# Last tile of tokens listed by a product of 0/1 rows on TensorE instead of by indirect DMAs, and the tile ahead of it routed inside attention's last values product

## What is computed

```
x = x + L0_xattn(layernorm(x), ctx, wq, wk, wv, wo)
x = x + L0_ffn(layernorm(x), w_gate, wi_0, wi_1, wo)        # 8 experts, 2 per token, I = 256
x = x + L1_xattn(layernorm(x), ctx, mask)                   # softmax(x ctx^T / sqrt(D)) ctx
x = x + L1_ffn(layernorm(x), gate_w, w_gate, w_up, w_down)  # 32 experts, 8 per token, I = 192

# a mixture of experts: logits -> top K -> weights; for a chosen expert
y = (silu(x @ gate_e) * (x @ up_e)) @ down_e                # weighted and summed per token
```

## Time and profile before

| | |
|---|---|
| median of 3 runs | 956.7 us (955.2 to 958.67) |
| the profiled execution's own time | 963.59 us |
| its span, first to last instruction | 961.8 us |
| TensorE matmul busy | 776.8 us (81%) |
| VectorE / ScalarE busy | 535.9 / 517.3 us |
| GpSimd busy | 455.7 us |
| `list_tokens` (L1013), all | 84.6 us in 80 indirect DMAs |
| mean granted TensorE clock | 0.927 of full speed |

### The profile page before, as it was taken

One profiled execution on the slowest core, in us unless ns is written; L12 is line 12 of the kernel. 1 busy time (PEld: TensorE's weight loads), 2 busy tenths in 40 slices (PEclk: granted clock), 3 DMA queues, 4 the chain that ended last, 5 costly groups with the idle time before them and its releaser, 6 DMA issues.

```text
span 961.8 us, 19102 instructions
## 1 busy us (share of the span) xinstructions
PE 776.8 (81%) x5216; PEld 433.3 (45%) x5217; DVE 535.9 (56%) x1504; ACT 517.3 (54%) x782; POOL 455.7 (47%) x373
## 2 busy tenths in 40 slices
PE   3999999999838989367699715989889889898880
PEld 2444455554424545134355303555555555555540
DVE  5553445565453555165688541674675764566642
ACT  6533244544445765223555423777687777677650
POOL 3882000000142667420067774566776766667760
PEclk9999999999958999779799856999999999999995
DMA  8562200100045797791111105799899999999778
GB/s 281 179 217 94 66 33 23 35 23 34 29 132 152 191 250 140 175 324 65 44 46 47 46 15 156 193 280 257 219 257 285 259 258 229 245 240 237 143 135 284
DMA packets 108780, 151.89 MB, mean 158 GB/s; under 512 B 18464, under 2 KB 59680, under 8 KB 108736
## 3 DMA queue, kind: packets, MB, share of 16 engines
...
...
...
## 4 chain that ended last, share of the span: by engine, by line
PE 48%; DMA 12%; issue 12%; DVE 12%; ACT 6%; DVEq 3%; ACTq 3%; POOL 2%; SPq 2%; POOLq 0%
PE pst L191 39%; DMA x_rows<-xT,row_no 4%; PE pst L1285 4%; DVE big L1172 3%; DMA big<-in_L_ffn_wo_dram 2%; PE pst L506 2%; DMA mid<-moe_normalised_rows,row_no 2%; POOL moe_tokens_of_experts L1013 2%; ACT mid L1321 1%; ACTq L1184 1%; DVE mid L1399 1%; DMA big<-x_rows 1%; ACT big L1165 1%; PE pst L1258 1%; DVEq L1177 1%
## 5 line engine op out<-in xcount | busy, mean ns | idle before, releaser
L191 PE MATMUL pst<-big,mid 128*128 (+1 forms) x1392 | 273.0, 347 | 39.7 <-DVE big L1172 24.0
L1013 POOL DMA_INDIRECT moe_tokens_of_experts<-token_no,small x80 | 84.6, 1057 | 274.0 <-DVE small L1066 253.9
L191 PEld LDWEIGHTS pst<-big,mid 128*128 128x128 f16 x1392 | 133.1, 98 | 146.5 <-issue 55.0
L1285 PE MATMUL pst<-big,mid 128*128 x520 | 129.9, 383 | 1.9 <-ACT mid L1332 1.4
L1321 ACT ACTIVATE mid<-pst 128x1024 f16<-128x1024 f16 x102 | 104.4, 1024 | 41.4 <-PE pst L1258 40.0
L1474 POOL DMA_INDIRECT x_rows<-mid,row_no x50 | 93.7, 1874 | 50.7 <-DMA x_rows<-xT,row_no 19.8
L1474 POOL DMA_INDIRECT x_rows<-xT,row_no x50 | 90.6, 1812 | 55.3 <-DMA x_rows<-mid,row_no 17.3
L1399 DVE SCALAR_TENSOR_TENSOR mid<-pst,small,mid 128x192 f32<-128x192 f32 (+1 forms) x100 | 42.7, 427 | 120.3 <-ACT mid L1327 120.2
L191 PE MATMUL pst<-ctxN,mid 128*128 128x512 f16 x384 | 91.8, 399 | 3.2 <-ACT mid L632 3.2
L1464 POOL DMA_INDIRECT xT<-moe_normalised_rows,row_no x54 | 59.6, 1104 | 37.4 <-issue 15.3
L1170 DVE TENSOR_TENSOR big<-big (+2 forms) x40 | 74.6, 1865 | 3.8 <-issue 0.2
...
## 6 DMA issues: line engine op xcount, KB each, us to landing
...
```

The lines of the kernel that those rows point to most:

```text
L191: last = nc.tensor.matmul(dst, stationary(a, c), moving(b, c), start=(k == 0), stop=(k == 3 * len(parts) - 1))
L1013: nc.gpsimd.indirect_dma_start(out=self.tab_d[:, :], out_offset=bass.IndirectOffsetOnAxis(ap=self.addr[j % 2][:, k:k + 1], axis=0), in_=to ...
L1285: last = nc.tensor.matmul(bank(6 + p), hT[:, k, :], self.d[:, s, h, c, :], start=(q == 0), stop=(q == len(seq) - 1))
```

## The change

- The listing by indirect DMA goes over tiles 0 to 6 only. Tile 7 is listed by a matrix product: `decode` takes each of its K addresses apart into a slot (a row of the table, 0 to 127) and a column; `slots_hot` makes K matrices 128 x 128 with the token's value where column number and slot agree, and zero elsewhere; `columns_hot` makes K matrices of 0/1 over the table's columns (64 in the first layer, 256 in the second); `list_last` multiplies them on TensorE and adds the K products up in PSUM bank 0. `tab16` becomes table plus this product. `table_sp` waits for the listings of three odd tiles instead of four.
- In the second layer, `logits` of tile 6 run behind 9 and `rank` of tile 6 behind 18 of the 24 matmuls of `values(7)`, instead of behind it and behind `norm_turn(7)`. VectorE's `choose`, `weight` and `place` of tile 6 stand ahead of `update(7)`. On ScalarE `soften(6)`, `store_weights(5)` and `store_weights(6)` stand ahead of `norm_high(7)`.
- In both layers `weight(7)` moves from ahead of `place(7)` to behind `columns_hot`; the four small operations on `ftab`, `ti` and `nquad` move behind the wait for `route_pe` 3; `sel` moves behind `tab16`; `split_lo(0)` moves behind the first four `rows_in_turn`.
- GpSimd's four stores of spare rows (L1487, L1488) move from behind the last listing to behind the listing of tile 0 (`spare_rows`).
- Constants: `tile_row` is 16-bit, `part_no` has a column more, `col_no` (column numbers, 16-bit) and `place_no` are new, `stats` has two rows instead of eight. The ring of raw weight buffers is as before.

```
-        tile_row = sb("tile_row", [P, 112], F32)
-        part_no = sb("part_no", [P, 2], F32)
+        tile_row = sb("tile_row", [P, 112], F16)
+        part_no = sb("part_no", [P, 3], F32)
         row_no = sb("row_no", [P, 8], I32)
-        spare16 = sb("spare16", [1, P], F16)
+        col_no = sb("col_no", [P, 2 * P], F16)
+        place_no = sb("place_no", [P, 3, 8], I32)
...
+        def three(pe, dst, parts, stationary, moving, pauses=None):
             k, last = 0, None
             for c in parts:
+                if pauses and c in pauses:
+                    pauses[c]()
...
+                    if not self.first and i == NT - 1:
+                        self.values(pe, i, {3: lambda: self.next.logits(pe, i - 1), 6: lambda: self.next.rank(pe, i - 1)})
+                    else:
+                        self.values(pe, i)
...
-                self.next.rank(pe, NT - 2)
+                if self.first:
+                    self.next.rank(pe, NT - 2)
                 self.next.logits(pe, NT - 1)
                 self.next.rank(pe, NT - 1)
...
+                else:
+                    self.next.soften(act, NT - 2)
+                    self.next.store_weights(act, NT - 3)
+                    self.next.store_weights(act, NT - 2)
+                    self.next.norm_high(act, NT - 1)
                     self.next.norm_move(act, NT - 1, self.norm_bank(NT - 1))
                 self.next.soften(act, NT - 1)
...
+                else:
+                    self.next.choose(dve, NT - 2)
+                    self.next.weight(dve, NT - 3)
+                    self.next.place(dve, NT - 2)
+                    self.next.weight(dve, NT - 2)
+                    self.update(dve, NT - 1)
+                    self.next.norm_row(dve, NT - 1)
+                    self.next.norm_low(dve, NT - 1)
                 self.next.choose(dve, NT - 1)
-                self.next.weight(dve, NT - 1)
                 self.next.place(dve, NT - 1)
...
-                    sp.wait_ge(self.listed[q], 16 * NT // 2 * self.K)
+                    sp.wait_ge(self.listed[q], 16 * (NT // 2 - q) * self.K)
...
+            def decode(self, dve):
+                L, K, src = self.E.bit_length() - 1, self.K, self.addr[(NT - 1) % 2][:, 0:self.K]
+                slot, col, rest = (place_no[:, r, 0:K] for r in range(3))
+                fslot, fcol, value = (place_no[:, r, 0:K].bitcast(F32) for r in range(3))
+                dve.wait_ge(self.addr_s, self.b + NT)
+                nc.vector.tensor_scalar(slot, src, L, P - 1, ALU.arith_shift_right, ALU.bitwise_and)
+                nc.vector.tensor_scalar(col, src, L + 7, L, ALU.arith_shift_right, ALU.logical_shift_left)
+                link(dve, nc.vector.tensor_scalar(rest, src, self.E - 1, None, ALU.bitwise_and))
+                nc.vector.tensor_copy(fslot, slot)
+                link(dve, nc.vector.tensor_tensor(fcol, col, rest, ALU.add))
+                link(dve, nc.vector.tensor_scalar(value, fslot, -1.0, part_no[:, 0:1], ALU.mult, ALU.add))
+            def slots_hot(self, dve):
+                for k in range(self.K):
+                    slot, value = (place_no[:, r, k:k + 1].bitcast(F32) for r in (0, 2))
+                    nc.vector.tensor_scalar(self.one_slot[:, k, :], col_no[:, 0:P], slot, value, ALU.is_equal, ALU.mult)
+            def columns_hot(self, dve):
+                for k in range(self.K):
+                    last = nc.vector.tensor_scalar(self.one_col[:, k, :], col_no[:, 0:NT * self.E],
+                                                   place_no[:, 1, k:k + 1].bitcast(F32), None, ALU.is_equal)
+                last.then_inc(self.rows_s, 1)
+            def list_last(self, pe):
+                pe.wait_ge(self.rows_s, 1)
+                for k in range(self.K):
+                    last = nc.tensor.matmul(bank(0)[:, 0:NT * self.E], self.one_slot[:, k, :], self.one_col[:, k, :],
+                                            start=(k == 0), stop=(k == self.K - 1))
+                last.then_inc(self.route_pe, 1)
...
+                self.list_last(pe)
                 pe.wait_ge(self.tab_s, 3)
                 nc.tensor.matmul(bank(4)[:, 320:320 + NE], ones16[0:1, :], self.crow, start=True, stop=True).then_inc(self.route_pe, 1)
-                pe.wait_ge(self.rows_s, 1)
+                pe.wait_ge(self.rows_s, 2)
                 for q in range(self.NQ):
...
             def dve_route(self, dve):
+                self.decode(dve)
                 dve.wait_ge(self.route_pe, 1)
                 nc.vector.tensor_scalar(self.nt16, self.cnt2, 1.0, None, ALU.max).then_inc(self.tab_s, 1)
+                self.slots_hot(dve)
                 dve.wait_ge(self.route_pe, 2)
                 link(dve, nc.vector.tensor_copy(self.incl, b4[0:E, 4:5]))
                 nc.vector.tensor_scalar(self.past, tile_row[0:E, :], self.incl, None, ALU.is_ge).then_inc(self.tab_s, 1)
+                self.columns_hot(dve)
+                self.weight(dve, NT - 1)
                 dve.wait_ge(self.route_pe, 3)
                 passed, earlier = b4[0:1, 64:64 + NE], b4[0:1, 192:192 + NE]
                 link(dve, nc.vector.scalar_tensor_tensor(self.colrow, earlier, -1.0, tile_row[0:1, :], ALU.mult, ALU.add))
                 link(dve, nc.vector.scalar_tensor_tensor(self.colrow, self.colrow, float(E), passed, ALU.mult, ALU.add))
+                nc.vector.memset(self.ftab[:, 0:3], 0)
...
                 nc.vector.scalar_tensor_tensor(self.crow, self.over, 4096.0, self.colrow, ALU.mult, ALU.add).then_inc(self.tab_s, 1)
+            def dve_rows(self, dve):
+                NE, b4 = self.NE, bank(4)
                 dve.wait_ge(self.route_pe, 4)
+                dve.wait_ge(self.tab_in, 32)
+                nc.vector.scalar_tensor_tensor(self.tab16, self.tab, float(-NT * P), bank(0)[:, 0:NT * self.E], ALU.add,
+                                               ALU.add).then_inc(self.rows_s, 1)
+                dve.wait_ge(self.route_pe, 5)
                 for q in range(self.NQ):
+                    nc.vector.tensor_scalar(self.sel[:, q, :], b4[:, 320:320 + NE], part_no[:, q + 1:q + 2], None, ALU.is_equal)
+                dve.wait_ge(self.route_pe, 6)
                 nc.vector.tensor_copy(self.tabT[0:self.CQ, :, :], bank16(3)[0:self.CQ, 0:self.NQ * P].rearrange("p (q s) -> p q s", q=self.NQ)).then_inc(self.rows_s, 1)
-                dve.wait_ge(self.route_pe, 6)
+                dve.wait_ge(self.route_pe, 7)
+                link(dve, nc.vector.tensor_scalar(self.rows, bank(5)[:, 0:NE], float(NT * P), None, ALU.add))
...
                 self.dve_route(dve)
-                self.split_lo(dve, 0)
                 self.dve_rows(dve)
                 for t in range(4):
                     self.rows_in_turn(dve, t, t)
+                self.split_lo(dve, 0)
...
+            def spare_rows(self, pool):
+                pool.wait_ge(self.before, 1)
                 for q in range(2):
                     pool.dma_start(acc_d[q][NT * P:NT * P + P // 2, :], x_sb[0:P // 2, 0, :]).then_inc(self.scat[q], 16)
                     pool.dma_start(acc_d[q][NT * P + P // 2:(NT + 1) * P, :], x_sb[P // 2:P, 0, :]).then_inc(self.scat[q], 16)
+            def pool(self, pool):
...
-            for j in range(NT):
+            for j in range(NT - 1):
                 exp0.list_tokens(pool, j)
+                if j == 0:
+                    exp0.spare_rows(pool)
```

68 lines of the change are left out of this document (29 added, 39 removed).

## The result

| | before | changed |
|---|---|---|
| median, timed side by side | 958.7 us (955.2 to 964.1, 8 runs) | 951.0 us (948.1 to 955.6, 8 runs) |
| the profiled execution's own time | 963.6 us | 951.7 us |
| its span | 961.8 us | 949.9 us |
| mean granted TensorE clock | 0.927 | 0.933 |

The ratio is 0.9915, interval 0.9891 to 0.9938: faster, by 7.7 us. The forecast was 12.7 us and 944.0, with a range to 949.0; the time lies outside it.

What follows compares the result with a forecast made beforehand. It took two holes between attention and experts as the target: GpSimd's listing in the second layer, VectorE's chain in the first. Gains of 11.4 + 1.3 = 12.7 us gave 950.9, less 0.7% 944.0 us; range 941.0 to 949.0.

Steps and rivals of the forecast that it cites:

- a term put at nothing: Next loads of weights, both layers: start 7.7 and 3.3 us later relative to the first gather, at no cost.
- Update(7) and the root: Second layer, VectorE: `update(7)` about 1.5 us later, the root's 1.28 us table load just hidden; 1.6 later in all.
- The table and VectorE: Second layer: table ready at 569.7, VectorE at 570.6, so VectorE last by 0.9; row numbers 12.6 us earlier.
- The one-hot operations: Second layer, VectorE: the 16 operations of `slots_hot` and `columns_hot` take 4.0 us, bounds 2.5 to 5.2.
- The shared port pair: Second layer: `slots_hot` and `columns_hot` hold tile 6's eighth listing at most 2.8 us; up to 945.9; 20% together with Dearer.
- Gathers beside `split_lo(0)`: Second layer: GpSimd's first gather is delayed 1.2 us by the moved split, with 0 to 2.9 possible.
- The first layer: Row numbers 2.1 us earlier, gather 1.3 lost, about 0.5 back from the next weights' load; 1.3 us gained in all.
- Dearer: VectorE's 16 operations take 5.2 us or more and splits hold gathers fully: 948.0 us; 20% together with The shared port pair.
- Cheap: VectorE's 0/1 operations take 2.5 us, the table is last and no gather is held: 942.5 us; 15%.
- The loop gives back: Experts' loop: weight loads sit otherwise against gathers and scatters, and late loads are waited for: 948 to 950 us; 10%.
- Slower than before: TensorE's clock falls after the idle matmuls because the first gather comes too late; five low-clock tiles cost 13 us; 3%.
- No change: The table still waits for something as late as tile 7's listing; VectorE would need 13 us more than counted; 2%.

Runs made afterwards that it cites:

- c_before: The kernel before with only the experts' list stored as 16-bit instead of 32-bit; ratios to before 1.0028, 1.0032 and 1.0025 in three sets.
- e_root_first: The changed kernel with 16-bit list, next round's loads held back, and `store_weights(6)` behind `norm_high(7)` in the second layer; 947.89 us, ratio 0.9878.
- e_early_split: The changed kernel with 16-bit list, next round's loads held back, and expert 0's splits early in the second layer; 943.43 us, ratio 0.9834.
- e_both: `e_early_split` with `store_weights(6)` also behind `norm_high(7)`; 966.58 us, ratio 0.9914, in a set about 15 us slower for every kernel.
- e_both2: The kernel of `e_both` measured again in the third set; 944.94 us, ratio 0.9832.

## Why the prediction was wrong

**The time.** By the stages the mechanism was right, and the change won 13.6 us where the sum has 12.7. The time was not: 7.7 us instead of 12.7, and 951.0 instead of 944.0. Two steps failed.

The first is the last of the sum, "The three runs have a median of 956.7, 0.7% under the profiled one, so I subtract there". Eight runs of before have 958.7, and the larger sets 960.9, 959.7 and 960.0: 2.0 us of the miss of 7.0 are this base. The range, 8 us wide, took in the rivals' costs and nothing for runs of one kernel that lie 9 us apart.

The second is a term put at nothing: "the next loads of weights ... are wanted only when an expert of the ring's next round is split, more than 15 us later". It asks when the data is needed, not what it travels beside. In the kernel before, the load stood behind the table's load in SyncE's list and went out 11.95 us ahead of the first gate matmul of the second layer; now `split_lo(0)` releases it 6.9 us ahead of it, upon the gathers. Held back, it gives 3.0 us by the stages, and the kernel has 948.5 us, inside the range. In the first layer the sum even took 0.5 us as a gain.

That the stages come to 13.6 all the same is in part luck: the 3.0 us are made up by row numbers that came 1.5 us earlier than forecast (13.5 against 12.6 in the second layer, 2.65 against 2.1 in the first) and by gates which, with the loads held, lie 0.2 us behind before's in the second layer and 0.6 ahead of them in the first, where the sum had 1.2 and 0.8 behind.

What is left of the miss, 5.0 us less in the difference of medians than the sum has, is not explained, for the stages, with the cost of the loads in them, won more than the sum. The difference of medians is 7.7 us in the first measurement, 9.2 and 10.7 in the later sets, 11.8 and 12.8 between controls that both have the 16-bit list, while the mean spans of the traces differ by 13.1. Of these 13.1, 2.4 are draws: the traced executions of before lie 4.9 and 2.7 us above and 1.8 below their kernel's median, those of the change 0.7 above, 3.0 below and 0.9 above. `c_before` was 0.25 to 0.32% over before in all three sets; no stage of its traces is longer for it, but of before itself there is only one trace, and a slow one. Why is open, and with it whether the real difference is nearer 8 or 13 us.

**Update(7) and the root.** Predicted 1.5 later, and the root's table load "just hidden", 1.6 in all. A root that its table load holds up was one of the prediction's signs of being wrong, and it came. Measured 0.45, and VectorE waited 1.22 us for the root where it had waited 0.27 (`e_root_first` undoes that). ScalarE in time, against the earlier trace rows:

```profile
553.78 0.32 ACT L1141 ACTIVATE big<-big,small 128x32 f32<-128x32 f32 x1 [1.90 <-DMA moe_normalised_rows<-big]
554.13 0.33 ACTq L1144 DMA_DIRECT2D moe_normalised_rows<-big  x1
554.49 1.28 ACT L305 ACT_TABLE_LOAD   x1 [0.39 <-ACT big L1141]
555.78 0.20 ACT L305 ACTIVATE std<-rstd 128x1 f32<-128x1 f32 x1
```

The store of tile 5's weights is waited for until 553.78 and the load ends at 555.77, which less 2.03 is 553.74, as forecast (554.0); but VectorE had the variance at 554.79, or 552.76, 1.1 us earlier than forecast, and waits. The sum of both, 1.4, is near the 1.6; that two terms of the wrong size add up to it is luck.

**The table and VectorE.** Tile 6's listing, the 1.26 us rhythm and the load 2.16 us behind the last listing came as forecast. VectorE was last in the changed kernel; with `e_root_first` the table is last by 0.59, so the two are level within a microsecond, as the sum had them (0.9). Row numbers 13.5 us earlier over three traces against 12.6: `columns_hot` ended at 569.19, or 567.16 less the 2.03, 0.9 earlier than forecast, most of it because the group itself took 1.64 us and not 2.4, while `slots_hot` took 0.4 more than forecast.

**The one-hot operations.** 3.66 us against 4.0, inside the bounds of 2.5 to 5.2. The parts are the other way about: operations of 128 columns with two pointers start 0.22 us apart, those of 256 columns with one pointer 0.20. In the first layer, with no listing beside them, the two-pointer ones again start 0.22 us apart and one-pointer ones of 64 columns 0.15: 192 columns more cost 0.05 us, or 0.26 ns each. The tiers of "VectorE: DVE Perf Modes" in the Trainium skill gave an estimate of 1.8 us. On the rate the trace agrees, for at the 0.96 GHz of that page 0.26 ns are four columns a cycle; the fixed part is what the estimate had too small (0.06 us, where the trace leaves 0.13 with one pointer and 0.19 with two).

**The shared port pair.** In the changed kernel this rival did not come: the listing issued at 566.38, within `slots_hot`, took 0.97 us. In the kernels where a listing began just behind the start of `columns_hot`, it took 1.35 to 1.55 us and ended with the group (above). For these one-pointer operations the trace agrees with the Trainium skill's "SBUF — State Buffer", on the engine ports, though the hold costs 0.4 to 0.6 us and not the 2.8 at most that the rival had; beside `slots_hot` the listings of all traces took 0.95 to 1.13.

**Gathers beside `split_lo(0)`.** The row of before was right. A gather that was issued beside the `tensor_tensor` took 1.62 us in the second layer and 2.13 in the first, and 0.99 with the split out of the way; a listing took 2.27 in before, 2.38 in `e_early_split`, 2.44 in `e_both` and 1.35 in `e_both2`. All six ended 0.27 to 0.31 us ahead of the end of the split's second half, whenever they had been issued, so the split holds them nearly to its end rather than slowing them by a fixed amount; a listing issued 0.03 us ahead of the split in `e_both2` took 0.96. The same page of the Trainium skill says, as an inference, that such an operation leaves descriptor writing alone; six measurements here differ. I took 1.2 us for the gather of the second layer, and the extra in the row is 0.6. The sum also left out that this gather goes out 1.24 us behind the row numbers, where it had been 1.77.

**The first layer.** Row numbers 2.65 us earlier (predicted 2.1), gate 0.85 later (predicted 0.8). The second number is right by luck: the load was to be a gain of 0.5 and cost 1.4, and with the loads held the gate lies 0.6 us ahead of before's, not 1.3 behind.

**Rivals.** *Dearer* did not come by its mechanism: the groups took 3.66 us, and the splits held the gathers nearly to their end, as this rival has it, but these went out so late into them that they lost 0.6 and 1.1; the measured 951.0 lies nearer its 948 than the forecast, but by another way. *Cheap* did not come either, VectorE was last. *The loop gives back*: the first loop +0.3, the second -0.6; not so. *Slower than before* did not come: the mean granted clock is 0.933 against 0.927. *No change* came in one set, at 0.998, by a way that was not among the rivals.
